# Attention probabilities times values in three rounded products instead of one fp32 product

## The reference

```
q, k, v, qx = fp8-rounded linear maps of layernorm(x)   # qx: queries of the cross type
kx, vx      = linear map of ctx
q, qx, k, kx = layernorm over the head dimension
p         = softmax(q k^T / sqrt(128))
y         = p v                                       # for both types
out       = x + tanh(g) * scale * (fp8(y / smooth) @ wproj^T)
```

## Time and profile before

| | before |
|---|---|
| median of 3 runs (lowest to highest) | 804.56 us (802.93 to 805.38) |
| the profiled execution's own time | 801.96 us |
| its span, first to last instruction | 800.1 us |
| TensorE matmul, busy | 718.0 us, 90% |
| TensorE weight load, busy | 582.8 us, 73% |
| VectorE, busy | 604.1 us, 76% |
| ScalarE, busy | 466.1 us, 58% |
| GpSimd, busy | 447.4 us, 56% |

### The profile page before, as it was taken

How to read it: one execution, slowest core, us unless ns; L and a number is a source line. 1 busy time by engine, 2 the same in 40 slices (tenths; PEclk the granted TensorE clock), 3 DMA queues, 4 the chain that set the end, 5 groups by cost and what they waited for, 6 DMA issues and landing times.

```text
span 800.1 us, 15318 instructions
## 1 busy us (share of the span) xinstructions
PE 718.0 (90%) x4857; PEld 582.8 (73%) x4857; DVE 604.1 (76%) x1286; ACT 466.1 (58%) x1179; POOL 447.4 (56%) x586
## 2 busy tenths in 40 slices
PE   3648899899999989999998999998978778999996
PEld 3546787788788778878877887887756556777775
DVE  6867888788888878888887888889888673444444
ACT  5646767677676767767666776866754322222221
POOL 3415777566777756677775667776766223222220
PEclk9979999999999999999999999999999897999999
DMA  5310100100010010001001010000010104666661
GB/s 185 112 53 1 53 3 1 54 28 28 0 45 10 1 54 27 27 1 40 16 1 54 1 34 2 27 1 2 1 42 19 67 9 132 195 190 189 192 186 54
DMA packets 44478, 42.74 MB, mean 53 GB/s; under 512 B 3717, under 2 KB 43386, under 8 KB 44410
## 3 DMA queue, kind: packets, MB, share of 16 engines
q1 hardware_dynamic: 41706, 36.61, 14.9%
q0 software_dynamic: 1536, 5.28, 2.5%
q10 hardware_dynamic: 1168, 0.01, 0.1%
HBM read 39.52 MB, written 2.37 MB: 52 GB/s over the span
## 4 chain that ended last, share of the span: by engine, by line
PE 63%; DVE 18%; ACT 6%; issue 6%; POOL 4%; DMA 1%; SPq 1%; POOLq 0%; DVEq 0%; ACTq 0%
PE out_ps L1748 9%; PE s_ps L1530 6%; PE proj_ps L1486 6%; PE proj_ps L1471 6%; PE pT_ps L1539 5%; DVE q_tok L1102 5%; PE aux_ps L1549 4%; PE aux_ps L1500 4%; PE aux_ps L1563 4%; PE proj_ps L1462 4%; PE work_ps L1740 3%; POOL rstd L528 3%; DVE pT_sb L1127 3%; DVE ss L1082 3%; PE work_ps L1762 2%
## 5 line engine op out<-in xcount | busy, mean ns | idle before, releaser
L543 POOL TENSOR_SCALAR p_sb<-p_sb,psum_row 128x256 f32<-128x256 f32 x256 | 125.0, 503 | 67.9 <-DVE psum_row L1121 66.6
L797 ACT ACTIVATE p_sb<-s_ps,negmax 128x256 f32<-128x256 f32 x256 | 118.3, 473 | 64.1 <-DVE negmax L1116 63.0
L1549 PE MATMUL aux_ps<-pT_sb,v_sb 128*128 128x512 f32 x256 | 120.7, 594 | 4.0 <-DVE pT_sb L1127 4.0
L1530 PE MATMUL s_ps<-kT,qT 128*128 128x256 f32 x768 | 112.3, 289 | 8.2 <-DVE qT L1112 4.6
L1127 DVE COPY pT_sb<-pT_ps 128x512 f32<-128x512 f32 x128 | 87.7, 686 | 41.3 <-PE pT_ps L1539 40.8
L550 POOL TENSOR_TENSOR y_bf<-y_bf,mg_bf 128x512 bf16<-128x512 bf16 x64 | 85.8, 1341 | 58.5 <-DVE mg_bf L1139 58.5
L1530 PEld LDWEIGHTS s_ps<-kT,qT 128*128 128x128 f32 x768 | 97.6, 190 | 18.3 <-issue 18.3
L1116 DVE TENSOR_REDUCE negmax<-s_ps 128x2 f32<-128x512 f32 x128 | 86.5, 683 | 5.9 <-PE s_ps L1530 5.6
L528 POOL TENSOR_TENSOR rstd<-var,minus_half 128x8 f32<-128x8 f32 (+1 forms) x64 | 85.7, 1339 | 5.3
L553 POOL TENSOR_TENSOR catq<-y_bf,mg_bf 128x512 fp32r<-128x512 bf16 x64 | 79.5, 1243 | 5.0
L1748 PE MATMUL out_ps<-eo,onehot 128*128 128x256 f32 x512 | 74.2, 297 | 0.6 <-ACT eo L909 0.6
(11 more groups left out here) (181 smaller groups left out, 1399.2 us busy)
## 6 DMA issues: line engine op xcount, KB each, us to landing
w_up_a<-in_L_ffn_gate_up_proj SPq DMA_DIRECT2D x16, 384.0 KB, 3.5
w_up_b<-in_L_ffn_gate_up_proj SPq DMA_DIRECT2D x16, 384.0 KB, 3.6
wp_raw<-in_L_xattn_wproj SPq DMA_DIRECT2D x16, 256.0 KB, 2.9
w_down_a<-in_L_ffn_down_proj SPq DMA_DIRECT2D x16, 192.0 KB, 3.5
w_down_b<-in_L_ffn_down_proj SPq DMA_DIRECT2D x16, 192.0 KB, 3.6
w_raw<-in_L_xattn_w_kv_x SPq DMA_DIRECT2D x8, 256.0 KB, 3.3
w_raw<-in_L_xattn_wq SPq DMA_DIRECT2D x7, 256.0 KB, 2.7
w_raw<-in_L_xattn_wqx SPq DMA_DIRECT2D x7, 256.0 KB, 2.9
```

Of the source, the lines that this page charges most:

```text
L543: ins = nc.gpsimd.tensor_scalar(p_sb[:, r, st, :], p_sb[:, r, st, :], rsum[:, r, st:st + 1], 1.0, ALU.mult, ALU.mult)
L797: ins = nc.scalar.activation(p_sb[:, r, st, :], s_ps[:, r % 2, st, :], ACT.Exp, bias=negmax[:, r, st:st + 1], accum_out=psum_row[:, r, st: ...
L1530: ins = nc.tensor.matmul(s_ps[:, k % 2, st, :], qT[:, a, ty, h, st * P:(st + 1) * P], kT[:, b, ty, s.gi, :], start=(i == 0), stop=(i == 2))
L1549: ins = nc.tensor.matmul(aux_ps[:, f.bank, :], v_sb[:, (2 * s.n + tt) % VRING, ty, s.gi, :], pT_sb[:, ty, :, tt, :], start=(tt == 0), stop ...
```

## The change

`p` and `v` are split as the other operands are: `y = p_hi v_hi + p_lo v_hi + p_hi v_lo`. ScalarE makes the high part of the turned probabilities (`pT_hi`), VectorE subtracts the low part (`pT_lo`, in place of `evac_pT`). ScalarE's copy of the values, which was there before, now writes a rounded tile, and VectorE subtracts `v_lo` (`v_low`, new). `pT_sb` keeps its size, but holds high and low parts of two blocks instead of four blocks. For the space, some tiles move: the first expert weights no longer have memory of their own during the attention, so all four pairs are loaded at its end; the layernorm's output goes into `sq`, the vectors into `mg_bf`, the first query weights into `k_tok`, one quantisation buffer into `q_tok`, with the waits that these need.

```diff
-        v_sb = sb("v_sb", [P, VRING, NTYPE, 2, D])
+        v_sb = sb("v_sb", [P, VRING, NTYPE, 2, D], F32R)
+        v_lo = sb("v_lo", [P, VRING, NTYPE, 2, D], F32R)
...
-        pT_sb = sb("pT_sb", [P, NTYPE, HPG, TPB, SEQ])
+        pT_sb = sb("pT_sb", [P, 2, HPG, TPB, SEQ], F32R)
...
@@ SP
-            sp.wait_ge(aux_filled, Fill("WQ", 1, 0).filled)
-            for u in range(2):
-                load_pair(u, u)
...
             sp.wait_ge(qk_normed, 2 * NSUB)
-            for u in range(2, RING):
+            sp.wait_ge(aux_filled, Fill("Vx", NSUB - 1).filled)
+            for u in range(RING):
                 load_pair(u, u)
...
@@ ScalarE, quant_y
+                if b == 1:
+                    act.wait_ge(h_ready, NB)
...
@@ ScalarE
+            def pT_hi(s, r):
+                act.wait_ge(pT_filled, s.m + (r + 1))
+                if r >= 2:
+                    act.wait_ge(aux_filled, Fill("Vs", s.a).filled)
+                elif s.a > 0:
+                    act.wait_ge(aux_filled, Fill("Vx", s.a - 1).filled)
+                nc.scalar.activation(pT_sb[:, 0, r % 2, :, :], pT_ps[:, r % 2, :, :], ACT.Copy).then_inc(pT_hi_ready, 1)
...
                 if kv:
                     squares_kv(*kv)
+                if s2:
+                    pT_hi(s2, 3)
                 if s1:
                     evac_Tq(s1, 1)
...
                 if s0:
                     squares_q(s0)
+                if s1:
+                    pT_hi(s1, 0)
+                    pT_hi(s1, 1)
...
                 if s0:
                     evac_Tq(s0, 0)
                     q_hi(s0, 0)
+                if s1:
+                    pT_hi(s1, 2)
...
@@ VectorE, ln_norm
+                wait(dve, hT_filled, b - 1)
...
@@ VectorE, scaled_kv
-                if n > 0:
-                    dve.wait_ge(aux_filled, Fill("TKx", n - 1).filled)
+                dve.wait_ge(aux_filled, Fill("TKx", n - 1).filled if n > 0 else Fill("WQ", 1, 0).filled)
...
@@ VectorE
-            def evac_pT(s, r):
-                dve.wait_ge(pT_filled, s.m + (r + 1))
-                if s.a > 0:
-                    dve.wait_ge(aux_filled, Fill("Vs" if r < 2 else "Vx", s.a - 1).filled)
-                nc.vector.tensor_copy(pT_sb[:, r // 2, r % 2, :, :], pT_ps[:, r % 2, :, :]).then_inc(pT_ready, 1)
+            def pT_lo(s, r):
+                dve.wait_ge(pT_hi_ready, s.m + (r + 1))
+                nc.vector.tensor_tensor(pT_sb[:, 1, r % 2, :, :], pT_ps[:, r % 2, :, :],
+                                        pT_sb[:, 0, r % 2, :, :].bitcast(F32), ALU.subtract).then_inc(pT_ready, 1)
+
+            def v_low(n, t):
+                at = 2 * n + t
+                dve.wait_ge(v_ready, at + 1)
+                nc.vector.tensor_tensor(v_lo[:, at % VRING, :, :, :].rearrange("p y g d -> p y (g d)"),
+                                        proj_ps[:, :, 2 * D:4 * D],
+                                        v_sb[:, at % VRING, :, :, :].rearrange("p y g d -> p y (g d)").bitcast(F32),
+                                        ALU.subtract).then_inc(v_lo_ready, 1)
...
                 if kv:
                     sums(kv_seq(*kv), 4)
+                if s2:
+                    pT_lo(s2, 3)
...
                 if kv:
                     scaled_kv(*kv)
+                    v_low(*kv)
...
                 if s1:
                     maxes(s1, 2)
-                    evac_pT(s1, 0)
+                    pT_lo(s1, 0)
...
                 if s0:
                     sums(q_seq(s0.a), 8)
                 if s1:
-                    evac_pT(s1, 1)
+                    pT_lo(s1, 1)
...
                 if s1:
-                    evac_pT(s1, 2)
+                    pT_lo(s1, 2)
                     magic(s1, 0)
...
-                if s1:
-                    evac_pT(s1, 3)
...
@@ TensorE, project_kv and project_q
-                wait(pe, v_ready, 2 * n + t)
+                wait(pe, v_lo_ready, 2 * n + t)
...
-                wait(pe, v_ready, min(s.a + 2, 2 * NU))
+                wait(pe, v_lo_ready, min(s.a + 2, 2 * NU))
...
@@ TensorE, fill_pv
+                pe.wait_ge(v_lo_ready, 2 * s.n + 2)
                 pe.wait_ge(pT_ready, s.m + 2 * (ty + 1))
                 for tt in range(TPB):
-                    ins = nc.tensor.matmul(aux_ps[:, f.bank, :], v_sb[:, (2 * s.n + tt) % VRING, ty, s.gi, :],
-                                           pT_sb[:, ty, :, tt, :], start=(tt == 0), stop=(tt == TPB - 1))
+                    for v, part in ((v_sb, 0), (v_sb, 1), (v_lo, 0)):
+                        ins = nc.tensor.matmul(aux_ps[:, f.bank, :], v[:, (2 * s.n + tt) % VRING, ty, s.gi, :],
+                                               pT_sb[:, part, :, tt, :], start=(tt == 0 and v is v_sb and part == 0),
+                                               stop=(tt == TPB - 1 and v is v_lo))
                 ins.then_inc(aux_filled, 1)
```

More of the change, by code:

```diff
@@ L66, in flamingo_kernel @@
         sdown_raw = w_raw[:, 5:7, 0:SI]
[L67 to L70, removed]
         wp_raw = sb("wp_raw", [P, 2, NTYPE, HPG * D])
@@ L80, in flamingo_kernel @@
         sq = sb("sq", [P, 8 * D])
-        vec_rows = sq[:, 0:P]
         vec = sb("vec", [P, 52])
@@ L105, in flamingo_kernel @@
         kT = sb("kT", [P, 2, NTYPE, 2, SEQ], F32R)
-        v_sb = sb("v_sb", [P, VRING, NTYPE, 2, D])
+        v_sb = sb("v_sb", [P, VRING, NTYPE, 2, D], F32R)
+        v_lo = sb("v_lo", [P, VRING, NTYPE, 2, D], F32R)
+        wq0_raw = k_tok[:, :, :].rearrange("p t a -> p (t a)").rearrange("p (r h) -> p r h", h=H)
         negmax = sb("negmax", [P, 4, TPB])
@@ L117, in flamingo_kernel @@
         ctx_raw = p_sb[:, :, :, :].rearrange("p a b c -> p (a b) c")
-        h_sb = pT_sb[:, :, :, :, :].rearrange("p a b c d -> p (a b c) d")
+        h_sb = sq[:, :].rearrange("p (n h) -> p n h", h=H)
+        vec_rows = mg_bf[:, :, :].rearrange("p a b -> p (a b)").bitcast(F32)[:, 0:P]
         stat = q_tok[:, 0, 0:6 * NT].rearrange("p (n k) -> p n k", k=6)
@@ L123, in flamingo_kernel @@
         q_y = [wp_raw[:, :, :, :].rearrange("p a b c -> p (a b c)").bitcast(BF16).rearrange("p (i k) -> p i k", k=SEQ),
-               v_sb[:, 3:5, :, :, :].rearrange("p a b c d -> p (a b c d)").bitcast(BF16)
-               .rearrange("p (i k) -> p i k", k=SEQ)]
+               q_tok[:, :, :].rearrange("p a b -> p (a b)").bitcast(BF16).rearrange("p (i k) -> p i k", k=SEQ)]
         q_mg = [qk_f[:, :, :].rearrange("p a b -> p (a b)").bitcast(BF16).rearrange("p (i k) -> p i k", k=SEQ),
@@ L146, in flamingo_kernel @@
         hxT = sm("hxT", [P, HC, T])
+        w_up_a = sm("w_up_a", [P, 2, 2, HC, I2])
+        w_down_a = sm("w_down_a", [I, 2, 2, H])
         w_up_b = sm("w_up_b", [P, 2, 2, HC, I2])
@@ L231, in flamingo_kernel @@
         pT_ready = sem("pT_ready")
+        pT_hi_ready = sem("pT_hi_ready")
+        v_lo_ready = sem("v_lo_ready")
         round_chain = sem("round_chain")
@@ L743, in evac_v @@
                 at = 2 * n + t
-                if at == 3:
-                    act.wait_ge(xq_ready, NB)
                 if at >= VRING:
@@ L965, in ln_norm @@
                 dve.wait_ge(rstd8_ready, b + 1)
+                wait(dve, hT_filled, b - 1)
                 for n in range(TPB * b, TPB * (b + 1)):
-                    ins = nc.vector.tensor_scalar(h_sb[:, n, :], x_sb[:, n, :], mv[:, n, 0:1], rs8[:, n:n + 1],
+                    ins = nc.vector.tensor_scalar(h_sb[:, n % 4, :], x_sb[:, n, :], mv[:, n, 0:1], rs8[:, n:n + 1],
                                                   ALU.subtract, ALU.mult)
@@ L1220, in _ @@
             scaled_kv(0, 0)
+            v_low(0, 0)
             wq_lo(0, 0)
@@ L1389, in transpose_h @@
                         ins = nc.tensor.transpose(s_ps[:, b % 2, c, tt * P:(tt + 1) * P],
-                                                  h_sb[:, TPB * b + tt, c * P:(c + 1) * P], ident[:, :])
+                                                  h_sb[:, (TPB * b + tt) % 4, c * P:(c + 1) * P], ident[:, :])
                 ins.then_inc(hT_filled, 1)
@@ L1589, in fill_fT @@
                     pe.wait_ge(qk_normed, 2 * NSUB)
-                    pe.wait_ge(v_ready, 2 * NU)
+                    pe.wait_ge(v_lo_ready, 2 * NU)
                     for c in range(HC):
```

## The result

The changed kernel takes **897.64 us** (median of 4 runs, 897.39 to 900.59); the kernel before, beside it, 803.74. The ratio is 1.118, with a 95% interval of 1.1162 to 1.1199: slower by 94 us. The prediction was 870, with a range up to 895. Direction and mechanism are there; the size is too small.

What follows compares the result with a forecast made beforehand. Bound: a latency loop through ScalarE, VectorE and GpSimd, close to TensorE's work. 31 periods growing from 17.47 to 19.55 give 64.5, start 1.2, draining some 2: 68 on 801.96, 870 us, range 848 to 895 (chance 0.68).

Steps and rivals of the forecast that it cites:

- Product: `fill_pv`: six rounded products replace four fp32 instructions, 1.41 for 1.72 us, 0.31 less a call; nothing taken for the end.
- step 1: pT(0): VectorE's sums wait behind `pT_lo(0)`, starting at 2.19 instead of 1.17; queries' transposes later, cost 1.02 us a period.
- step 2: pT(2): `magic` and the low query half queue behind `pT_lo(2)`; low half at 10.96 instead of 8.41, 2.55 with step 1.
- Step 3: Keys: GpSimd's reciprocal root, behind its rounding, sets `scaled_kv`, which runs at 15.31 in place of 13.01.
- Step 4: `project_q` waits for `v_low`, queued behind `scaled_kv`, and ends at 18.6 instead of 15.92; 2.7 us per plain iteration.
- The plain iteration: Attention loop period without weight fills: 18.6 us, or 19.2 in the other kind, where `kT` is subtracted too.
- The weights' 0.65: Weight fills in the attention loop: 5.2 us left on the loop in eight iterations, 0.65 each.
- The draining iterations: Two iterations at the attention's end, in which pT still passes two engines: some 2 us.
- Start and loads: Two `v_low` before the first `project_q` cost 1.2 us; expert weight loads at the attention's end, covered by 48 us, cost nothing.
- TensorE keeps the pace: Rival: sums in the loop do not wait, the shorter product shows, 20 us less, 782; chance 0.06.
- Only the first step is paid: Rival: later steps in the loop find slack, 0.7 more per period, about 827, up to 848; chance 0.14.
- The clock falls: Rival: TensorE, idling more in the loop, drops its clock to about 0.8; 900 to 930 us; chance 0.10.

Runs made afterwards that it cites:

- the run with three orders and without `v_low`: Changed kernel with sums before pT_lo(0), magic(0) and qk_lo(TQ) before pT_lo(2), x1_stats behind pT_lo(3), v_low and its product left out: 816.61 us.

## Why the prediction was too low

In the terms of the sum: the 31 periods rose by 84.3 us and not by 64.5, what lies behind them by 10.2 and not by 2, and the start by 1.1, not 1.2. The mechanism held; two terms were too small. With only one of them wrong the time would have stayed inside the stated range: with the order at the end changed back it was 889.95.

**Product.** The call takes 434.36 + 0.40 - 433.12 = 1.64 us. In the same view, which counts the last matmul to its end, the call of the kernel before takes 1.88:

```profile
392.06 1.88 PE L1549 MATMUL aux_ps<-pT_sb,v_sb 128*128 128x512 f32 x4
```

So the product got 0.24 shorter, not 0.31. (The prediction's 1.41 and 1.72 are pieces of the chain, which leave out overlap.) The step's verdict, that nothing comes of it because waits hide the call, holds: with a third of the matmuls nothing was gained.

**Steps 1 and 2** hold to about a hundredth of a microsecond in the rows, though undoing them gave back less than they had added, 0.81 of 1.02 and 0.98 of 1.53 a period. One sign was missed: TensorE idles 1.07 in front of the transposes, not 1.5 to 2, because 0.66 of the wait now stand in front of the product, which waits for `pT_lo`. **Step 3**, that GpSimd's rounding sets `scaled_kv`, holds in five of the iterations, the only ones in which VectorE waits there. **Step 4** holds in kind. `v_low` ends last ahead of `project_q` (17.0 us of TensorE's idle time).

**The plain iteration was sized too low: the first failing term.** The prediction had 18.6 and 19.2; the rows give 453.77 - 434.54 = 19.23, and the other kind is 19.8. Of the 0.63 in this iteration the rows account for 0.61: GpSimd's reciprocal root for the keys takes 1.35 instead of 1.02, 0.33 (step 3); `project_q` starts 0.15 after `v_low`, which was taken as nothing, and takes 2.13, which was taken as 2.0. In the other kind the keys' low half takes 1.65 instead of 1.35. 0.6 a period is 19 us in 31. The weights' 0.65 was about right in sum: between the 9th and the 25th `scaled_q` the mean period is 20.04, or 0.54 above the mean of the two plain kinds. That is partly luck. The plain kind with the long reciprocal root comes five times in 31, and two iterations in eight, which do have weight fills, take only 18.9 and 19.0.

**The draining iterations were the second: 2 us predicted, 10 measured.** The 2 us rested on no row. They were for pT passing two engines, not for what else `pT_lo(3)` moved past. `evac_pT(s1, 3)` stood ahead of `x1_stats` in VectorE's order; `pT_lo(s2, 3)` stands behind it, and three products waited 3.5 to 4.2 us. Undoing that alone put "behind" back to 207.2, about the predicted 205.4 + 2. The mean over all 31 periods is also 0.15 above that of the 16 in the middle, 4.6 us, mostly two long ones near the end (24.2 and 22.7 us); moving `x1_stats` shortened them by 1.1 in all. In the kernel before the same two were the longer ones as well, 18.9 and 18.3; why they grew by more than the others is open. Together 19 - 3 (the weights, 0.11 less) + 8 + 5 = 29 us, against the 28 by which the profiled execution is above the forecast.

**Start and loads** hold: 1.1 for 1.2, and no run shows a late expert weight. ScalarE is busier by 56 us and not 77, VectorE by 16 and not 22; neither entered the sum. The range was wider than its reason: half a microsecond in each of 31 periods is 15.5 us, and 848 to 895 is 22 down and 25 up.

**The rivals.** *TensorE keeps the pace* is refuted by the products taken out and added: at the same clock the periods of the run with two matmuls a call equal those of the run with six. The Trainium skill ("Perfetto Trace Analysis", Identifying the Most-Contended Engine) would have one optimize the engine with the highest occupancy first, and judge TensorE's headroom by its weight loads. TensorE is still highest, at 82% by matmuls and 70% by weight loads, and less work on it made 919: what limited it were its waits. *Only the first step is paid* is refuted by step 2's 33 us. *The clock falls* didn't happen in the loop, where the changed kernel has 1.00 in the 300 us from 200 to 500, but it did at the end, around the three waits of about 4 us, and in the loop of two experiments that took work from TensorE.

So of the 94 us the orders of step 1, step 2 and `x1_stats` are 65, `v_low` with its product 16, and 13 remain unassigned.

## What to carry to other kernels

Where a loop of latencies and a busy engine lie close together, price a change by the place of each new instruction in each engine's order: which instruction is queued behind it, and who waits for that. A low part that nobody needs yet belongs behind the sums and roundings that the loop waits for; three such moves were worth 65 of 94 us here, while ScalarE's added load was worth none. When an instruction is moved over an iteration's edge, look also at what stands there only in the last iterations.

## What was not expected of the hardware

Some of VectorE's subtractions with both operands in SBUF and some of GpSimd's instructions hold each other up. In the changed kernel, from 60 to 680 us, the low halves of L1127 last 0.67 to 0.69 or about 1.65 us, nothing between. All 15 long ones start while GpSimd runs L549, as in the rows here, where the one ends 0.54 us after the other. In the kernel before, the same 15 start 0.3 us later within the same GpSimd instruction, and take 1.35. The other way round, 5 of 30 reciprocal roots of the keys take 1.33 to 1.35 instead of 1.02, and these are the five at whose start such a subtraction was running; none of 30 before.

```profile
420.19 1.65 DVE L1127 TENSOR_TENSOR kT<-qk_f,kT 128x512 fp32r<-128x512 f32 x1
```

```profile
419.76 1.54 POOL L549 TENSOR_TENSOR y_bf<-y_bf,mg_bf 128x512 bf16<-128x512 bf16 x1 [2.88 <-DVE mg_bf L1161]
```

The kernel before, GpSimd, for the subtraction at 372.78 in the earlier trace rows:

```profile
372.04 1.54 POOL L550 TENSOR_TENSOR y_bf<-y_bf,mg_bf 128x512 bf16<-128x512 bf16 x1 [1.36 <-DVE mg_bf L1139]
```

Not every meeting costs: 20 low halves in the changed kernel start while GpSimd runs a reciprocal root (L527), and still take 0.67 to 0.69.

The Trainium skill ("SBUF — State Buffer", SBUF: two separate sides) says that a VectorE instruction with two SBUF inputs and a GpSimd instruction that reads SBUF take a shared pair of ports in turn, whoever starts first holding it to its end. The durations at L549 agree; the 20 at L527 do not, so the rule doesn't hold for every GpSimd instruction here. No run was made to test it. These longer durations are in both kinds of the plain iteration: by being shifted in time, the same instructions met others.

This is also a candidate for the 13 us that are left. With the low query half ahead of `pT_lo(2)`, it starts within GpSimd's rounding. In the run with three orders and without `v_low`, 45 of the 96 low halves last over 0.9 us, and what all of them take beyond 0.68 adds up to 28.1 us; in the kernel before it is 15, and 10.2 us. One iteration of it, GpSimd and then VectorE:

```profile
269.70 1.17 POOL L549 TENSOR_TENSOR y_bf<-y_bf,mg_bf 128x512 bf16<-128x512 bf16 x1 [0.56 <-DVE mg_bf L1161]
270.95 1.49 POOL L552 TENSOR_TENSOR catq<-y_bf,mg_bf 128x512 fp32r<-128x512 bf16 x1
```

```profile
269.87 1.54 DVE L1127 TENSOR_TENSOR qT<-qk_f,qT 128x512 fp32r<-128x512 f32 x1 [0.26 <-ACT qT L781]
...
271.94 1.05 DVE L1127 TENSOR_TENSOR kT<-qk_f,kT 128x512 fp32r<-128x512 f32 x1
```

The two take 2.59 us, where they took 0.69 + 1.35 = 2.04 in the kernel before, and the period is 17.18 against 16.51. How much of it is paid, no run shows.
